# First sample's taps mixed by float32 products from whole weights, the pieces brought into float16 parts one by one in later epochs

## The reference

```python
g = _gn(x)                                   # 32 groups of 8 channels, eps 1e-5
pooled = jnp.mean(g, axis=(2, 3))
att = jax.nn.sigmoid(pooled @ att_w.T + att_b)
agg_w = jnp.einsum('nk,kocij->nocij', att, weight)      # a 3x3 weight of its own per sample
out = x + conv3x3(g, agg_w)                  # per sample, stride 1, padding 1
```

## Time and profile before

| | us |
|---|---|
| three runs | 1335.6, 1336.1, 1336.32 (median 1336.1) |
| the profiled execution | 1336.13 |
| its span | 1334.0 |
| TensorE matmuls busy | 1268.9 (95%) |
| VectorE busy | 1206.3 (90%) |
| ScalarE busy | 915.1 (69%) |
| TensorE's matmuls of L450 / L415 | 1158.7 / 105.8 |
| VectorE's `w_low` (L861) in the first 64 us | 8 passes |

### The profile page before, as it was taken

How to read it: one execution, slowest core, us unless ns; L and a number is a source line. 1 busy time by engine, 2 the same in 40 slices (tenths; PEclk the granted TensorE clock), 3 DMA queues, 4 the chain that set the end, 5 groups by cost and what they waited for, 6 DMA issues and landing times.

```text
span 1334.0 us, 23201 instructions
## 1 busy us (share of the span) xinstructions
PE 1268.9 (95%) x8744; PEld 726.9 (54%) x8744; DVE 1206.3 (90%) x2112; ACT 915.1 (69%) x1441; POOL 56.3 (4%) x72
## 2 busy tenths in 40 slices
PE   0299999999999999999999999999999999999998
PEld 0055555555555555555555555555555555555555
DVE  8899899999899999989999998999989999998983
ACT  4986576766767686776777767677776767667531
POOL 0000000000000000000000000000000000000000
PEclk9899999999999999999999999999999999999999
DMA  9201535545253553525455352545525255552434
GB/s 374 107 1 44 146 102 146 145 97 153 67 156 111 146 146 79 157 77 149 122 146 145 74 146 79 148 137 146 146 58 152 82 145 146 130 153 58 102 95 142
DMA packets 29324, 165.17 MB, mean 124 GB/s; under 512 B 3360, under 2 KB 3616, under 8 KB 28192
## 3 DMA queue, kind: packets, MB, share of 16 engines
q1 hardware_dynamic: 20288, 113.94, 23.1%
q0 software_dynamic: 8928, 49.78, 22.2%
HBM read 112.33 MB, written 51.38 MB: 123 GB/s over the span
## 4 chain that ended last, share of the span: by engine, by line
PE 94%; DVE 2%; DMA 2%; ACT 1%; SPq 1%; issue 0%; DVEq 0%
PE pM L450 86%; PE pG L415 7%; DMA Us<-w_dram 2%; DVE W L861 1%; ACT W L1084 0%; DVE E L609 0%; PE pS L403 0%; SPq L382 0%; DVE Us L618 0%; DVE T L603 0%; SPq L344 0%; ACT Vs L991 0%; ACT L1069 0%; DVE Vs L623 0%; DVE X L722 0%
## 5 line engine op out<-in xcount | busy, mean ns | idle before, releaser
L450 PE MATMUL pM<-Vs,Us 128*128 128x385 f16 (+1 forms) x6912 | 1158.7, 330 | 1.8 <-DVE Us L618 1.8
L450 PEld LDWEIGHTS pM<-Vs,Us 128*128 128x128 f16 x6912 | 672.9, 98 | 484.6 <-issue 14.8
L991 ACT CAST Vs<-E 128x784 f16<-128x784 f32 x192 | 159.7, 840 | 118.3 <-DVE E L595 56.2
L570 DVE SCALAR_TENSOR_TENSOR T<-X 128x392 f32<-128x392 f32 x384 | 193.3, 558 | 15.7 <-ACT X L1040 14.0
L623 DVE TENSOR_TENSOR Vs<-E,Vs 128x784 f16<-128x784 f32 x192 | 182.3, 967 | 2.6 <-ACT Vs L991 2.4
L415 PE MATMUL pG<-W,D 128*32 128x512 f16 x1728 | 105.8, 391 | 40.2 <-DVE W L861 40.2
L1002 ACT CAST Us<-E 128x768 f16<-128x768 f32 x128 | 101.7, 828 | 40.1 <-DVE E L609 40.1
L595 DVE SCALAR_TENSOR_TENSOR E<-T 128x784 f32<-128x784 f32 x128 | 119.1, 972 | 2.2
L618 DVE SCALAR_TENSOR_TENSOR Us<-E,Us 128x768 f16<-128x768 f32 x128 | 118.9, 951 | 0.1
L609 DVE SCALAR_TENSOR_TENSOR E<-G,T 128x768 f32<-128x768 f32 x128 | 116.9, 954 | 2.2
L1060 ACT ACTIVATE unused<-X,small 128x784 bf16<-128x784 f32 x120 | 113.8, 948 | 4.1 <-ACT small L1056 0.3
(11 more groups left out here) (79 smaller groups left out, 569.1 us busy)
## 6 DMA issues: line engine op xcount, KB each, us to landing
X<-x_dram SPq DMA_DIRECT2D x66, 784.0 KB, 5.4
out_dram<-X SPq DMA_DIRECT2D x64, 784.0 KB, 3.7
X<-x_dram POOLq DMA_DIRECT2D x62, 784.0 KB, 8.3
W<-w_dram SPq DMA_DIRECT2D x6, 1152.0 KB, 17.4
Us<-w_dram SPq DMA_DIRECT2D x2, 1152.0 KB, 25.4
attw<-attw_dram SPq DMA_DIRECT2D x1, 128.0 KB, 8.6
small<-attb_dram SPq DMA_DIRECT2D x1, 0.5 KB, 9.7
```

The source lines that it names most:

```text
L450: mm = pe.matmul(tile_rows(bank(k, o))[:, :, first:last], Us[:, j, a, c, o, kx, :], v_in(j, b, c, kx), start=(at < 2 and i == 0), stop=(i ...
L570: ins = dve.scalar_tensor_tensor(out=dst[c], in0=a[c], scalar=scale, in1=d[c], op0=ALU.mult, op1=ALU.add)
L991: act.copy(v_out(j, 0), e_buf(n, ("V", chunk, j))).then_inc(v_hi, 1)
```

## The change

The first sample's mix no longer needs split weights. All eight pieces land in W32 and stay there in float32. `mix_tile` multiplies a piece that isn't split yet by a float32 product with D32, one product for each j and tile (two for the tile that takes the ends of both halves), and the split pieces by three float16 passes as before; the float32 products of a tile come first, j by j. For sample 0, D32 is unscaled and the scale ws comes in with `u_high` and `u_low`, which read it from `first_scale` and wait for `us_set`; for later samples `attention` multiplies D32 by ws in one more step while pieces are still whole.

One piece is split in each of epochs 1 to 8 (`SPLIT`: pieces 0, 4, 1, 5, 2, 6, 3, 7). ScalarE's queue issues a copy of the piece within SBUF to G, which is free between the last `u_low` of the sample and the next `take_taps`; `w_high` reads it there ahead of `root`, `w_low` reads it after the second `add_rows` of slot 3, behind `attention`. `mix(n + 1, 0)` and the first `take_taps` wait for w_lo. So the mixes of samples 0 and 1 are wholly float32, that of sample 2 has one split piece, and so on; from sample 9 on all are float16.

The lists of epoch 0 are in new orders. ScalarE's begins: root, two norms, bias, exponential, w_sum 2, w_sum 3, v_high 3, tap 0, v_high 4, tap 1, v_high 1, w_sum 5, taps 2 and 3, w_sum 4, w_sum 7, tap 4, w_sum 6, v_high 2, tap 5, v_high 5, taps 6 to 8, u_high of (0,0), (0,1), (0,2), (0,5), (1,2), (1,1), (1,0), then sums(1,1,0,0), u_high (0,3), (1,3), (0,4). VectorE's, after its two norms: v_pair of points 3 and 4, attention, v_pair of 1 and 2, v_low 3, v_low 4, w_max 1, v_single 5, w_max 0, v_low 1, u_pair(0,0,1), w_bound, v_low 2, w_scale, v_low 5, unscales, u_pair(0,1,1), u_low of (0,2), (0,1), (1,2), (1,1), u_pair of both halves for 3 and 4, u_low (0,3), (1,3), v_single 0, u_low (0,0), (0,4), a v_pair of the lower rows, v_low 0, u_low (1,0), take_other, u_low (1,4). The rest of epoch 0, and the order tables that the counts of semaphores use, follow these lists.

```diff
--- before.py
+++ after.py
@@ -128,7 +128,9 @@
 SUMS = [(0, 0), (0, 1), (1, 0), (1, 1)]
 SHIFTS = [c for chunk, c in SUMS if chunk == 0]
-MAXED = [0, 1]
+MAXED = [1, 0]
+SPLIT = ((), (0,), (4,), (1,), (5,), (2,), (6,), (3,), (7,))
 NE, NV, NU = len(E_NEXT), len(V_LO_NEXT), len(U_LO_NEXT)
 NA, ND = len(ACT_TAKES), len(DVE_TAKES)
 EB = 4
...
@@ -213,11 +217,11 @@
         W16 = W32[:, :, :, :].bitcast(F16)
-        Us32 = Us[:, :, :, :, :, :, :].rearrange("p j s c o k n -> p (j s c o k n)").bitcast(F32)
-        w_piece = ([W32[:, i // JT, i % JT, :] for i in range(2, CT * JT)]
-                   + [Us32[:, WG * i:WG * (i + 1)] for i in range(2)])
-
-        G16 = G[:, :, :, :, :].rearrange("p c o k n -> p (c o k n)").bitcast(mybir.dt.bfloat16)
+        w_piece = [W32[:, i // JT, i % JT, :] for i in range(CT * JT)]
+        w_aside = [G[:, :, :, :, :].rearrange("p c o k n -> p (c o k n)")[:, WG * i:WG * (i + 1)] for i in range(2)]
+        Us16 = Us[:, :, :, :, :, :, :].rearrange("p j s c o k n -> p (j s c o k n)").bitcast(mybir.dt.bfloat16)
...
@@ -332,6 +337,13 @@
         def dve_count(n, takes):
             order = LAST if isinstance(n, int) and n == N - 1 else DVE_TAKES
             return n * ND + max(order.index(t) for t in takes) + 1
+
+        def split_in(n):
+            return SPLIT[n] if n < len(SPLIT) else ()
+        def split_before(n):
+            return sum((split_in(i) for i in range(n)), ())
...
             def mix_tile(n, m):
                 if not is_first(n) or m >= MIX_BANKS:
                     pe.wait_ge(taps_taken, n * TAKES + m - MIX_BANKS + 1)
+
+                done = split_before(n)
+                halves_of = range(CT) if m == FULL else (0 if m < FULL else 1,)
+                dst = [pG[CI * j:CI * (j + 1), m % MIX_BANKS, :] for j in range(JT)]
+                if m == FULL:
+                    dst = [d.rearrange("p (c n) -> p c n", c=CT) for d in dst]
+                for j in range(JT):
+                    for c in halves_of:
+                        if JT * c + j not in done:
+                            one = W32[:, c:c + 1, j, :] if m == FULL else W32[:, :, j, :]
+                            mm = pe.matmul(dst[j][:, c:c + 1, :] if m == FULL else dst[j], D32[:, :], mix_part(one, m),
+                                           start=True, stop=True, tile_position=(0, CI * j))
                 for a, b in ((0, 0), (0, 1), (1, 0)):
                     for j in range(JT):
-                        dst = pG[CI * j:CI * (j + 1), m % MIX_BANKS, :]
-                        if m == FULL:
-                            dst = dst.rearrange("p (c n) -> p c n", c=CT)
-                        mm = pe.matmul(dst, D[:, a, :], mix_part(W16[:, :, j, b * WG:(b + 1) * WG], m),
-                                       start=(a == 0 and b == 0), stop=(a == 1), tile_position=(0, CI * j))
+                        mine = [c for c in halves_of if JT * c + j in done]
+                        if mine:
+                            parts = W16[:, :, j, b * WG:(b + 1) * WG]
+                            if m == FULL:
+                                parts = parts[:, mine[0]:mine[-1] + 1, :]
+                            mm = pe.matmul(dst[j][:, mine[0]:mine[-1] + 1, :] if m == FULL else dst[j], D[:, a, :],
+                                           mix_part(parts, m), start=(a == 0 and b == 0), stop=(a == 1),
+                                           tile_position=(0, CI * j))
                 mm.then_inc(mixed, 1)
             def mix(n, u):
                 if u == 0:
                     pe.wait_ge(att_ready, n + 1)
+                    if split_in(n - 1):
+                        pe.wait_ge(w_lo, len(split_before(n)))
                 for m in range(MIX_BANKS * u, MIX_BANKS * (u + 1)):
                     mix_tile(n, m)
...
             def keep_clock(n):
+                j = V_HI[0][0][1]
+                pe.wait_ge(v_hi, 1)
                 for _ in range(n):
-                    pe.matmul(pS[:, P:P + TAPS], W16[:, 0, 0, 0:P], W16[:, 0, 0, 0:TAPS], start=True, stop=True)
+                    pe.matmul(pS[:, P:P + TAPS], Vs[:, j, 0, 0, 0:P], Vs[:, j, 0, 0, 0:TAPS], start=True, stop=True)
             pe.wait_ge(small_in, 32)
             logits_mm(0)
             pe.wait_ge(att_ready, 1)
-            pe.wait_ge(w_lo, JT)
+            for i in range(JT):
+                pe.wait_ge(w_in[i], 16)
             mix_tile(0, 0)
             mix_tile(0, 1)
             mix_tile(0, 2)
             mix_tile(0, 3)
-            pe.wait_ge(w_lo, CT * JT)
+            for i in range(JT, CT * JT):
+                pe.wait_ge(w_in[i], 16)
             mix_tile(0, 4)
             mix_tile(0, 5)
...
-            logits_mm(1)
             group(0, 5, 1)
             group(0, 6, 0)
+            logits_mm(1)
             group(0, 6, 1)
-            mix(1, 0)
             group(0, 7, 0)
             group(0, 7, 1)
+            group(0, 8, 0)
+            mix(1, 0)
+            group(0, 8, 1)
             mix(1, 1)
-            group(0, 8, 0)
-            group(0, 8, 1)
-            mix(1, 2)
             group(0, 9, 0)
             group(0, 9, 1)
+            mix(1, 2)
             group(0, 10, 0)
             group(0, 10, 1)
             group(0, 11, 0)
...
                     src, scale = G[:, c, :, 0 if j == 0 else 2, :], U_0 if j == 0 else U_INF
                 else:
                     src, scale = halves(e_buf(n, ("U", c, j))), 1.0
+                if is_first(n):
+                    dve.wait_ge(us_set, 1)
+                    i = {0: 1, 5: 2}.get(j, 0)
+                    scale = first_scale[:, i:i + 1]
                 dve.scalar_tensor_tensor(out=u_flat(j, 1, c), in0=src, scalar=scale, in1=u_flat(j, 0, c),
                                          op0=ALU.mult, op1=ALU.subtract).then_inc(u_lo, 1)
...
                 dve.wait_ge(exp_ready, n + 1)
                 step(dve.tensor_scalar(ex1[:, :], ex[:, :], 1.0, None, ALU.add))
                 step(dve.reciprocal(att[:, :], ex1[:, :]))
-                step(dve.tensor_scalar(D32[:, :], sel[:, :], att[:, 0:1], ATT_SCALE, ALU.mult, ALU.mult))
                 if not is_first(n):
                     dve.wait_ge(mixed, n * TAKES)
-                step(dve.tensor_copy(D[:, 0, :], D32[:, :]))
-                dve.tensor_tensor(D[:, 1, :], D32[:, :], D[:, 0, :], ALU.subtract).then_inc(att_ready, 1)
+                ins = dve.tensor_scalar(D32[:, :], sel[:, :], att[:, 0:1], ATT_SCALE, ALU.mult, ALU.mult)
+                whole = len(split_before(n)) < CT * JT
+                if not is_first(n):
+                    step(ins)
+                    step(dve.tensor_copy(D[:, 0, :], D32[:, :]))
+                    ins = dve.tensor_tensor(D[:, 1, :], D32[:, :], D[:, 0, :], ALU.subtract)
+                    if whole:
+                        step(ins)
+                        ins = dve.tensor_scalar(D32[:, :], D32[:, :], ws[:, 2:3], None, ALU.mult)
+                ins.then_inc(att_ready, 1)
             def take_other(n, k, o):
...
                 if more:
                     attention(n + 1)
                 add_rows(n, b, 3, 1)
+                if len(split_in(n)) > 0:
+                    w_low(n, 0)
                 if more:
                     v_pair(n + 1, 1 - b, 0, 1)
                     v_pair(n + 1, 1 - b, 0, 3)
...
             def unscales():
                 dve.wait_ge(scale_set, 1)
                 step(dve.reciprocal(ws[:, 3:4], ws[:, 2:3]))
+                for i, scale in enumerate((1.0, U_0, U_INF)):
+                    dve.tensor_scalar(first_scale[:, i:i + 1], ws[:, 2:3], scale, None, ALU.mult)
                 for i, scale in enumerate(US):
                     ins = dve.tensor_scalar(us[:, i:i + 1], ws[:, 3:4], scale, None, ALU.mult)
                 ins.then_inc(us_set, 1)
-            def w_low(i):
-                if i == 0:
-                    dve.wait_ge(scale_set, 1)
-                dve.wait_ge(w_hi, i + 1)
-                dve.scalar_tensor_tensor(out=W16[:, i // JT, i % JT, WG:2 * WG], in0=w_piece[i], scalar=ws[:, 2:3],
+            def w_low(n, at):
+                i = split_in(n)[at]
+                dve.wait_ge(w_hi, len(split_before(n)) + at + 1)
+                dve.scalar_tensor_tensor(out=W16[:, i // JT, i % JT, WG:2 * WG], in0=w_aside[at], scalar=ws[:, 2:3],
                                          in1=W16[:, i // JT, i % JT, 0:WG], op0=ALU.mult,
                                          op1=ALU.subtract).then_inc(w_lo, 1)
-
-            STEPS = 36
...
@@ -995,11 +1030,15 @@
                     slot_done(n - 1, NC + ORDER.index(j))
                 if j in (0, 5):
                     act.wait_ge(taps_taken, n * TAKES + TILE_TAKES[c])
-                    act.mul(u_flat(j, 0, c), G[:, c, :, 0 if j == 0 else 2, :],
-                            U_0 if j == 0 else U_INF).then_inc(u_hi, 1)
+                    src, scale = G[:, c, :, 0 if j == 0 else 2, :], U_0 if j == 0 else U_INF
                 else:
```

(83 more changed lines are left out.)

164 lines of the change are left out of this document (79 added, 85 removed), and 8 rows, old and new, of the table E_FIRST.

## The result

The changed kernel takes 1337.9 us (median of 20 runs, 1337.5 to 1339.0) against 1335.5 for the kernel before (20 runs, 1334.5 to 1336.9): 1.0018 times as long, with a 95% interval of 1.0012 to 1.0024. It is slower by 2.4 us: the interval leaves out 1, but the difference lies just under the 0.2% (2.7 us) that the prediction named as what can be told from nothing. The profiled execution took 1337.87 us, its span 1335.7, against 1334.0 of before. Of a start made 23.9 us shorter nothing is left, and the trace says where it went.

The account below looks back on a forecast made before the run. TensorE, nearly all convolution matmuls, was taken as the bound. Start -23.0, mixes +16 and wait +11 gave +4 on 1336.1, stated as 1340.5 us; its own range 1331 to 1348, the full range 1320 to 1394.

Parts of the forecast that it names:

- Start: Epoch 0: without the splitting passes, group 1 starts at 61.4 us instead of 84.41, worth -23.0 us, 4 either way.
- replay: Epoch 0's new lists worked through with durations of before: us_set 47.4, group 0 at 53.9, group 1 at 61.4 us.
- cost nothing: Epoch 0, TensorE: keep_clock products ending some 2 us ahead of group 0 were said to add no time.
- the 1.4 us that group 1 would wait for its u_low: Epoch 0, TensorE: group 0 ends at 60.0, VectorE's u_low at 61.4, so group 1 waits 1.4 us.
- Mixes: Mixes of samples 1 to 8: 68 tiles with whole pieces at 0.23 us more each, +15.6, put at +16 us.
- Four passes and side by side: Float32 mix products: each costs four float16 passes, column tiles overlapping, so a tile lasts 0.92 us instead of 0.69.
- drains: Where mix units end: an allowance that took the mixes' +15.6 us to +16, with 2 us of the range.
- The wait: First mix unit of the next sample, epochs 1 to 8: TensorE waits 1.4 us for w_low, +11 us in all.
- the rival with no wait: Next sample's first mix: VectorE reaches attention over 1.4 us earlier against TensorE, so no wait; 1329 us, chance 0.11.
- ScalarE's part at nothing: Epochs 1 to 8: w_high falls into ScalarE's 3.25 us idle before root, the copy should be there; costs nothing.
- Partly serial float32: Mixes: strict program order makes whole pieces run partly one after another, +60 us; 1387 us (1378 to 1398), chance 0.28.
- Two passes: Mixes: a float32 product costs only two float16 passes, eight mixes 2 us less than before; 1322 us, chance 0.12.

Follow-up runs that it names:

- mix_later: Changed kernel with the next sample's first mix unit behind group (8, 0) in epochs 1 to 8: 1328.6 us, 0.9945 times the kernel before.
- low_first: Changed kernel with w_low ahead of attention instead of behind the second add_rows: 1330.0 us, 0.9955 times the kernel before.

## Why the prediction came out as it did

Forecast 1340.5, measured 1337.9, in the direction and by the mechanism given. The direction is less sure than the terms: +2.4 us is the difference of terms of 24 and 26 us. The sum itself has a slip: -23.0 + 16 + 11 = +4 on 1336.1 is 1340.1, not 1340.5. Term by term:

- **Start, -23.0 forecast, -23.9 measured.** Group 0 came at 52.7 (53.9 in the replay) and group 1 at 60.5 (61.4). The replay's order was right and about a microsecond long in VectorE's list. One sentence was wrong: the warming products that end 2 us ahead of group 0 "cost nothing". Group 0 ran in part at the lower clock. The sum was saved by another step, the 1.4 us that group 1 would wait for its u_low: the slow group fell into this wait, and with the full clock the wait appeared (1.37 us). The prediction did not see that, so for this sentence the right sum is luck.
- **Mixes, +16 forecast, +15.1 measured.** Four passes and side by side were both right: a unit of 2.8 was forecast, 2.71 (chain) to 2.82 (timeline) came. A pass added 0.22 us a tile (15.1 over 68 tiles) where 0.23 was taken from the float16 unit; the drains added nothing. The choice rested on one row, the logits' loads of 191 ns. The float32 matmul records themselves last 590 ns against 379 for float16, and there are two of them for a product against three: 1.18 us of records against 1.14, so records alone wouldn't have given the price, the units do. The Trainium skill, "FP8 and Floating Point Precision", section TensorE Precision Notes, has four passes for true FP32; the units agree (0.90 us a tile against 0.69 for three).
- **The wait, +11 forecast, +10.6 measured,** at its place and with its cause: 1.36 against 1.4. Taking it away gave back 9.3 us of the 10.6 (mix_later), and shortening it by 1.0 gave back 7.9 (low_first), of the 8 expected. "VectorE reaches attention earlier", the rival with no wait, did not occur.
- **ScalarE's part at nothing** was right for one piece: the copy landed 5.6 us after its issue, w_high did not wait for it (166.56), and root still came only when VectorE was ready. With two pieces it was no longer free.
- **Partly serial float32** was given 0.28, too much. Its condition, matmuls held back in program order, is what the exchanged loops show not to happen in float16, and the float32 units show the same by their length. The Trainium skill's "TensorE: Matmul & The Clock Gate", in "The mechanism" of its packing part, has matmuls strictly in order at start and end; taken so that a blocked column tile blocks the next, that gives 1387 us here, and the trace speaks against this reading (2.15 us tile by tile, 2.12 round the tiles).
- **Two passes** fell with the units of 2.7 to 2.8 us; 1.4 would have been seen.

The difference of 2.6 us is made of 0.9 at the start, 0.9 in the mixes, 0.4 in the waits, and the 0.4 of the slip. The medians differ by 2.4 us and not by the 1.8 of the terms because the profiled execution of before (1336.1) was above the median of its 20 runs (1335.5).

## What to carry to other kernels

Price a moved step at the place where its last consumer waits, not by its engine's idle time: w_low was free by VectorE's load and cost 1.36 us an epoch by its position, and moving either it or its reader by one step gave most of the time back. Work put off from a start is paid once in every later epoch in which it is unfinished, so the sum runs over the epochs; here doing it in fewer epochs, with each wait at the tile that reads the piece and ScalarE's list not held up by the copies, was worth nearly 8 us more (1328.6 to 1320.9), while doing it in fewer epochs alone lost 7 (1337.9 to 1345.3). Before a wait of TensorE is let grow, add what the clock takes behind it.

## What the runs showed of the hardware that was not expected

- Waits of 3.6 to 5.2 us left TensorE at a granted clock of 0.50 for 6 us in one case and some 3 to 5 in the others; filling them with unread products was worth 9.9 us over four, 2.5 each. A wait of 1.36 us, as in epoch 1 of the changed kernel, left its window at 1.00. At the start 2.2 to 2.9 us of idle time was followed by a lower clock in four of the six versions of the changed kernel with 40 products (0.79 and 0.59 in the changed kernel itself), and 2.47 and 2.57 us by 1.00 in the other two.
- Passes of one column tile issued in a row run beside those of the next tiles as well as when they are issued round the tiles: 2.15 and 2.12 us for 36 float16 matmuls.
- A copy of 1.18 MB within SBUF took 5.6 us from issue to landing in the median of eight; issued two at a time the median was 7.8, and the one shown took 8.89.
